# A post-norm transformer block on one core: the window's steps in a new written order, and the causal mask in one product

## The reference

```
qkv    = x @ Wqkv                                   # 16 heads of 16
logits = q k^T / 4 + slope[h] * (j - i), and -inf where j > i
x      = layernorm(x + softmax(logits) v @ Wout)
h      = silu(x @ wg^T) * (x @ wu^T)                # 768 hidden, weights int32 * 1/127
x      = layernorm(x + h @ wd^T)
```

## Time and profile before

| | |
|---|---|
| median of 3 runs | 1958.27 us (1955.96 to 1960.21) |
| span of the profiled execution | 1954.4 us; no time of its own outside the span is recorded for it |
| PE busy | 1867.6 us (96%), 18276 matmuls |
| PEld | 1436.9 us (74%) |
| DVE | 1477.3 us (76%) |
| ACT | 1186.9 us (61%) |
| POOL | 1092.4 us (56%) |
| DMA | 299.27 MB, 153 GB/s in the mean |

### The profile page before, as it was taken

The page is one execution under the profiler, slowest core; times in us unless marked ns, Lnnn a source line. Parts: engine busy times, 40 slices in busy tenths (PEclk is TensorE's granted clock), DMA queues, the critical chain, the costliest instruction groups (busy, mean ns, idle before and its releaser), DMA issues.

```text
span 1954.4 us, 46531 instructions
## 1 busy us (share of the span) xinstructions
PE 1867.6 (96%) x18276; PEld 1436.9 (74%) x18276; DVE 1477.3 (76%) x2521; ACT 1186.9 (61%) x1999; POOL 1092.4 (56%) x2052
## 2 busy tenths in 40 slices
PE   5789999999999999999999999999999999999987
PEld 4556777777777777777787787777787777777676
DVE  5667787777778777778777778877778777778745
ACT  1656666566666666666666666666666666666553
POOL 0234665565565565565565565555565555566566
PEclk7999999999999999999999999999999999999998
DMA  6464554454454444445445455445454455444320
GB/s 221 148 200 142 166 161 148 161 160 153 158 158 159 155 155 159 155 156 166 148 155 175 142 168 161 143 163 165 145 171 157 143 168 163 144 165 150 112 78 28
DMA packets 167931, 299.27 MB, mean 153 GB/s; under 512 B 33920, under 2 KB 88960, under 8 KB 155136
## 3 DMA queue, kind: packets, MB, share of 16 engines
q1 hardware_dynamic: 167520, 295.24, 46.2%
q10 hardware_dynamic: 192, 1.05, 0.2%
HBM read 175.64 MB, written 119.54 MB: 151 GB/s over the span
## 4 chain that ended last, share of the span: by engine, by line
PE 77%; DVE 11%; ACT 7%; POOL 1%; issue 1%; DMA 1%; SPq 1%; POOLq 0%; DVEq 0%; ACTq 0%
PE pair L573 75%; ACT probs L799 5%; DVE row_max L878 4%; DVE row_max L881 4%; DVE x1t_lo L866 2%; PE pair L576 2%; ACT x1t_hi L779 1%; ACT pv_t L807 1%; DVE row_max L883 0%; SPq L514 0%; DMA q_rows<-max_lo 0%; POOL h_lo L1004 0%; DMA probs<-L_attn_Wqkv 0%; POOL x L1030 0%; DVE staged_lo L866 0%
## 5 line engine op out<-in xcount | busy, mean ns | idle before, releaser
L799 ACT ACTIVATE probs<-pair 128x1024 f32<-128x1024 f32 x640 | 620.8, 1030 | 317.1 <-PE pair L573 316.7
L997 POOL TENSOR_SCALAR_AFFINE_SELECT probs<-probs 128x256 f32<-128x256 f32 (+1 forms) x896 | 380.2, 440 | 641.5 <-ACT probs L799 634.4
L1004 POOL TENSOR_TENSOR h_lo<-h_fulls,h_hi 128x256 fp32r<-128x256 f32 x384 | 277.5, 741 | 112.9 <-ACT h_hi L831 109.9
L573 PE MATMUL pair<-probs,v_ones 128*32 128x512 f32 (+3 forms) x4096 | 328.5, 439 | 4.3 <-ACT probs L799 1.5
L573 PE MATMUL pair<-q_rows,k_rows 64*128 64x512 f32 (+3 forms) x2048 | 315.2, 366 | 10.0 <-DMA q_rows<-max_lo 2.0
L881 DVE TENSOR_REDUCE row_max<-pair 128x2 f32<-128x1024 f32 x256 | 312.4, 1220 | 12.6 <-PE pair L573 8.0
L573 PE MATMUL pair<-k_rows,q_rows 63*128 63x512 f32 (+3 forms) x2048 | 297.3, 347 | 22.4 <-DVE row_max L881 15.0
L883 DVE TENSOR_REDUCE row_max<-pair 128x8 f32<-128x1024 f32 x256 | 311.9, 1218 | 0.0
L573 PEld LDWEIGHTS pair<-k_rows,q_rows 63*128 63x128 f32 x2048 | 165.7, 186 | 167.9 <-DVE row_max L881 81.2
L878 DVE TENSOR_REDUCE row_max<-pair 128x4 f32<-128x1024 f32 x128 | 156.9, 1226 | 124.0 <-PE pair L573 124.0
L823 ACT ACTIVATE h_fulls<-pair 128x256 f32<-128x256 f32 x384 | 144.9, 377 | 147.8 <-PE pair L573 145.6
(11 more groups left out here) (89 smaller groups left out, 3281.6 us busy)
## 6 DMA issues: line engine op xcount, KB each, us to landing
q_rows<-bounce SPq DMA_DIRECT2D x192, 256.0 KB
k_rows<-bounce SPq DMA_DIRECT2D x192, 256.0 KB
bounce<-staged_hi SPq DMA_DIRECT2D x128, 256.0 KB, 2.5
bounce<-staged_lo SPq DMA_DIRECT2D x128, 256.0 KB, 2.8
pv_bounce<-pv_t SPq DMA_DIRECT2D x128, 256.0 KB, 2.0
x_sb<-L_attn_x SPq DMA_DIRECT2D x32, 512.0 KB, 4.5
attn<-pv_bounce SPq DMA_DIRECT2D x64, 256.0 KB
recips<-recip_bounce SPq DMA_DIRECT2D x64, 256.0 KB
```

The costliest lines, as they stand in the source:

```text
L573: return tensor.matmul(o, lhs, rhs, start=start, stop=stop, skip_group_check=True, **kw)
L799: scalar.activation(probs[g][:, tile, :, :], pair[:, :, :], ACT.Exp, scale=scale).then_inc(s_exp, 1)
L997: made = pool.affine_select(out=diagonal, in_=diagonal, compare_op=ALU.is_ge, fill=0.0, base=0, pattern=[[0, diagonal.shape[1]], [1, P]], ...
L1004: pool.tensor_tensor(h_lo[:, m, :], h_full[(n_split_h[step] - 1) % H_BUFFERS][:, :], h_hi[:, m, :].bitcast(F32), ALU.subtract).then_inc(s_ ...
```

## The change

The class's `attention` and `rest` are replaced by two tuples, `SEQUENCES`, one for even windows and one for odd ones. A token is a step with its number; "<" in front means that it belongs to the window before (so "<down" in window w is the down of window w-1). There are five differences:

1. The attention stretch now has, between groups of F and S tiles, whole dense steps: both projections of the next unit and the down of the previous window. These were at the end of the rest. The weighted sums are whole (`PV_PARTS` has one part for each group), not in two pieces.
2. All banks go by last use: an F, S or V takes the pair used longest ago, whichever it is, and so do single steps; the pair in which a weighted sum is under way is left out.
3. A V waits for each block's own tile (`LAST_TILE`), not for the last tile of its group.
4. The exponential of H steps (`scores_halved`: two S tiles of an even window, three of an odd one) is two instructions of 512 columns instead of one of 1024, and the next user of each bank waits for its own half.
5. The mask is one product for a whole 128-column block: `turned` and `stair` use powers of two so that 64 rows describe 128 columns. There are two products per tile instead of four, of 128 or 256 columns.

```diff
-PV_PARTS = ((0, 1), (1, 4))
-ATTENTION = ((S, 0), (F, 0), (S, 1), (F, 1), (V, -2, 1, 0), (F, 2), (S, 2), (F, 3), (V, -2, 1, 1), (S, 3), (F, 4), (S, 4),
-             (F, 5), (S, 5), (F, 6), (S, 6), (F, 7), (V, -1, 0, 0), (F, 8), (S, 7), (V, -1, 0, 1), (S, 8), (F, 9), (S, 9))
+PV_PARTS = (((0, 1, 2, 3),), ((0, 1, 2, 3),))
+LAST_TILE = (2, 3, 4, 3)
+SEQUENCES = (
+    (
+        "F 0", "<project 0", "<fetch_recip", "F 1", "S 0", "<load_residual", "<second_norms", "S 1", "V 2 1 0", "S 2", "F 2", "S 3",
+        "F 3", "S 4", "<project 1", "S 5", "F 4", "F 5", "<down", "H 6", "F 6", "S 7", "F 7", "V 1 0 0", "gather", "store_max 0",
+        "divide", "H 8", "S 9", "F 8", "F 9", "combine", "x 0", "gate_up 0", "gate_up 1", "attn_split", "gate_up 2", "x 1",
...
+    ),
+    (
+        "<norm1_later 2", "<project 0", "F 0", "F 1", "H 0", "V 2 1 0", "S 1", "F 2", "S 2", "F 3", "norms", "<stats1 2", "S 3", "S 4",
+        "<project 1", "S 5", "F 4", "F 5", "<down", "<norms", "H 6", "S 7", "F 6", "F 7", "V 1 0 0", "H 8", "F 8", "S 9", "divide",
+        "F 9", "gather", "store_max 1", "x1 0", "x1 1", "store_max 0", "recip", "values 0", "combine", "max_row 0", "values 2",
...
+    ),
+)
...
+    def oldest_pair(self):
+        return min((i for i in range(BANKS // 2) if i != self.held), key=lambda i: max(self.used[2 * i:2 * i + 2]))
...
-                    for c in range(2):
-                        made = both(lambda s: halves[:, s, masked, c, :], lambda r: turned[r:r + HALF, c, :],
-                                    lambda r: stair[r:r + HALF, 0:n, :], False, c == 1)
+                    made = both(lambda s: diagonals[:, s, masked, :], lambda r: turned[r:r + HALF, :],
+                                lambda r: stair[r:r + HALF, 0:n, :], False, True)
...
-                    e.wait_ge(s_select, n_select["select", u, g * TILES + TILES - 1])
                     e.wait_ge(s_values, n_values["values_out", b, 2])
-                    for j in range(*PV_PARTS[part]):
+                    for j in PV_PARTS[g][part]:
+                        e.wait_ge(s_select, n_select["select", u, g * TILES + LAST_TILE[j]])
...
+                    if (u, i) in plan.halved:
+                        for s in range(2):
+                            scalar.activation(probs[g][:, tile, s, :], pair[:, s, :], ACT.Exp, scale=scale).then_inc(s_exp, 1)
```

More of the change, by code:

```diff
@@ L90, in __init__ @@
         self.order, self.norms_due, self.stats_due = [], [], []
-        self.banks, self.before = {}, {}
+        self.banks, self.before, self.halved = {}, {}, set()
         self.user, self.used = [None] * BANKS, list(range(-BANKS, 0))
-        for w in range(-2, self.units + 5):
-            self.attention(w)
-            self.rest(w)
+        for w in range(-2, self.units + 6):
+            self.held = None
+            for token in SEQUENCES[w % 2]:
+                what, *key = token.lstrip("<").split()
+                STEPS[what](self, w - token.count("<"), *map(int, key))
         self.second_norms()
@@ L103, in occupy @@
         self.banks[step] = banks
-        self.before[step] = list(dict.fromkeys(self.user[i] for i in banks if self.user[i] is not None))
+        self.before[step] = [(self.user[i], i % 2) for i in banks if self.user[i] is not None]
         for i in banks:
@@ L118, in norms, with combine, gather, divide @@
         self.norms_due = []
-    def second_norms(self):
+    def combine(self, w):
+        if self.has(w):
+            self.add("combine", w)
+    def gather(self, w):
+        if self.has(w + 1):
+            self.add("gather", w + 1)
+    def divide(self, w):
+        if self.has(w - 3):
+            self.add("divide", w - 3)
+        if w == 0:
+            self.add("load_ffn_weights")
+    def max_row(self, w, with_ffn):
+        if self.has(w) and with_ffn == (self.ffn(w) is not None):
+            self.split("max_row", w)
@@ L121, in second_norms @@
+    def second_norms(self, w=None, with_ffn=None):
+        if with_ffn is not None and with_ffn != (self.ffn(w) is not None):
+            return
         for b, part in self.stats_due:
@@ L125, in second_norms @@
         self.stats_due = []
[L127 to L174, removed]
-        for c in range(2):
[L176 to L201, removed]
-                self.add("split_h", b, part, m - 1)
-    def down(self, b, part):
-        self.take("down", b, part)
-        self.add("residual2", b, part)
-        self.stats_due.append((b, part))
@@ L239, in rest, with recip @@
             self.add("attn_lo", w - 3)
-        if part == 1 and has_ffn:
-            self.max_row(w)
-        if has_ffn and self.has(w):
-            self.add("store_max", w)
+    def recip(self, w):
         if self.has(w - 2):
@@ L461, in bank_emptied @@
             if step[0] == "scores":
-                return s_exp, n_exp[("exp",) + step[1:]]
+                return s_exp, 2 * n_exp[("exp",) + step[1:]] - (side == 0 and step[1:] in plan.halved)
             return s_lo, n_lo[("split_lo",) + step]
@@ L585, in _ @@
                 kind, key = step[0], step[1:]
-                for user in plan.before.get(step, []):
-                    e.wait_ge(*bank_emptied(user))
+                for user, side in plan.before.get(step, []):
+                    e.wait_ge(*bank_emptied(user, side))
                 if kind in ("x", "x1"):
```

234 lines of the change are left out of this document (142 added, 92 removed), and 2 rows, old and new, of the table SEQUENCES.

## The result

The changed kernel takes 1898.53 us in the median (1897.17 to 1901.88, 4 runs) against 1958.26 (1955.96 to 1960.21): the ratio is 0.970, 95% interval 0.9686 to 0.9713. Forecast was 1900. The profiled execution's span is 1900.1 us. That is the slowest of its four executions, 1.6 us above the median, while the span before, 1954.4, is 3.9 us under its median; so the two spans lie 54.3 us apart and the medians 59.7.

What follows compares the result with a forecast made beforehand. PE waiting in a DVE-PE bank chain in attention, alternating with PE alone in the rest, was taken as the bound; 0.97 us a window over 60 windows gave 58 us, 1958 - 58 = 1900 us (own range 1873 to 1928; 8 in 10: 1862 to 1946).

Steps and rivals of the forecast that it cites:

- The bound: Attention stretch: a chain between DVE's reads and PE's bank refills; 10.65 us of PE work takes 13.64, 2.99 waits and restarts.
- The sum of a window: Stretches of 18.4 us, rests of 9.3 and 9.4, plus 0.4 a window: 56.3 us a pair against 58.24.
- borders: Changes between tiles and other work in the new stretch: five pieces at 0.2 us, 1.0 a window, giving 17.35 without waits.
- The walk: Pass through a pair of windows in the changed order of waits and bank releases: stretches end at about 18.4 us.
- Whole sums: Weighted sums whole, V waiting by block: nothing for itself, as the group's last tile is several tiles earlier anyway.
- Halves: Exponentials in two halves: 0.4 us more on ACT a window, banks free 0.5 us earlier; -10 to +10 us by itself.
- Mask: Mask merged from 2560 products to 1280 with the same columns: +2 to -5 us, taken as 0.
- Banks by age: Every bank given by last use, as the walk assumed; no size of its own was forecast.
- Start and end: First and last windows: the down comes one window later, which matters only for the last; plus or minus 6 us.
- third rival: Gather lands late for F 0, slower than before: 1993 us; chance 0.09, shared with any other new hold-up.
- the waits did not come back elsewhere: Rival for the new stretch: tile groups pay another 0.15 us each, only 14 us gained, 1944; chance 0.17.
- One sign: DVE in the attention stretch: no idle of over 1 us, with its busy share up to about 78%.

Runs made afterwards that it cites:

- dense_back: Changed kernel with both projections and the down of each window set one behind the other ahead of the first F: 1998.1 us, 1.0211 of the kernel before.
- early_start: Changed kernel with projections of units 0 to 6 still at the end of the window two ahead, from unit 7 as changed: 1884.2 us.
- dense_and_banks: Kernel before with banks by age, and both projections and the down between the tiles from window 6 on: 2045.7 us, 1.0451 of the kernel before.
- v_split: Changed kernel with each weighted sum in two pieces again, S and F tiles between them: 1973.6 us, 1.0091 of the kernel before.
- banks_back: Changed kernel with the old bank rule, two pairs fixed for F, two for S and V: 2168.2 us, 1.1085 of the kernel before.

## Why the prediction was right, and where it was not

**The bound.** Right in the main: PE was held by the readers in the attention stretch, and the weight loads' waits for row maxima fell from 159.5 to 18.2 us. That in this order of tiles the dense work between them does this is borne out by dense_back, which takes it out and loses 3.6 us a pair, more than the whole gain, with 64.9 and 23.6 us of weight loads' waits for maxima back. The size, 2.99 us a window of waits and restarts, stood on a price of 0.233 for an S tile that was taken from a projection. The prediction's own rows have an S at 1028.62 - 1028.30 = 0.32, and the changed kernel has 0.32 (1008.09 - 1007.77) and, behind a projection, 0.34 (1011.66 - 1011.32). For ten such tiles that is some 0.9 us a window, an estimate, that was counted as waits and did not go away.

**The sum of a window.** Right: 56.10 us for a pair against 56.3, with both stretches (18.54 and 18.47 against 18.4) and both rests near; the four are 0.60 us over their bare sums, where 0.8 was allowed. In the parts it is less good. A whole sum is 2.29 us and not 2.43, 0.28 less a window. With it, the bare pieces of a stretch are 16.35 - 0.28 = 16.07 us, so borders and waits together, priced at 1.0 and some 1.05, were 18.54 - 16.07 = 2.47; the two errors partly cancel. Most of the 2.47 are no waits that show: the one recorded on PE in the odd stretch holds it by 0.46 - 0.04 = 0.42 us. The price of a gap ahead of other work is as estimated: 1012.43 - 1012.27 = 0.16 us from the mask to the down, against 0.04 to a tile.

**The walk.** It is on record with its results and not step by step, so it can't be shown which of its steps gave the value, and 0.8 of its 56.3 us are an allowance. Its waits for ACT are in the trace, at S 4 in the even window and at S 3 instead of S 4 in the odd one. The waits of 0.2 to 0.3 at F 9 and the first step of the rest are not recorded as waits of PE.

**The single edits** are where the prediction failed, behind a right total. Whole sums: "nothing for itself", measured 75 us for their undoing. Halves: within -10 to +10, measured 28.3. Mask: 0, bounds +2 to -5, measured 5 to 8, just outside. Banks by age: counted as a help inside the walk, it is the condition of the new order (270 us) and nothing without it (0.9993). The step that went wrong here is that I priced edits as if they added up. Undone one at a time they cost 3, 6.5, 28, 75, 100, 100 and 270 us, of a gain of 60. In the traces of the five dearest PE waits for readers of banks that the changed kernel does not wait for, or not as long: each one's price is that of an order in which some bank comes round before its reader is done.

**Start and end.** The forecast had 56 windows at 0.97 and half of that for eight more. The trace has 48 windows at 1.07, and 3.0 us in all for the other 16, where the forecast had some 11.6. "Plus or minus 6" was wrong in the parts: some 7 us net lost up to the ninth unit, and about 10 gained behind the 57th, when the 5 us of place are taken out of both. That the total of the medians is met within 1.5 us is in part luck: more in each steady window, less at the ends, and 54.3 us between the spans, in which the 58 were reckoned.

What PE waits for at the start is the third rival's mechanism: too little work between the issue of a gather and the F 0 that needs it, five waits up to 7.7 us, in windows that have no gate_up to cover it. I had looked for it only in the steady part. early_start puts the projections back between the two and takes 12.9 us of these waits and 14.3 us of the time away. Whether the late projection also delays the gather's issue is not shown.

**The rivals.** In the steady part the gather is not waited for, the waits did not come back elsewhere, and some of them stay. ACT's busy time rose by 17.8 us (25 forecast). DVE's busy share of the execution is 77% (78% forecast). One sign failed: no idle of DVE above 1 us was to be in a stretch, and there is one of 1.12 us in the odd and of 1.26 and 1.62 us in the even one.

**What stays open.** Why dense_and_banks loses 88 us is seen in its waits, but not resolved step by step. Of v_split's 75 us the two causes were not separated. Where half of the shorter mask's gain goes, and whether the dense work between tiles gains in any other order of tiles, was not found out.

## What to carry to other kernels

Where a chain between PE and the readers of PSUM alternates with a stretch of PE alone, put the one into the other; but the order and the assignment of banks are one decision. Take the built program, list for each step whose read it waits for, and walk a period with measured durations: that gave 56.3 us for 56.10 here, with 0.8 of allowance in it, while prices for single edits were wrong by 28 and 75 us in the prediction, and by some 230 in the expectation for banks_back. After a reordering look at the filling windows by themselves, since they lack the work that covers a transfer in the steady ones.

## What the runs showed of the hardware that was not expected

From the start of a bf16 mask product of 256 columns to the start of the next float32r product there are 0.04 to 0.05 us where no wait holds it (1011.95 - 1011.90), while 256 columns take 0.12 us in a projection (half of 1.40 / 6). So a distance across such a change of type is not the time of the product in front. Why it is so short is not shown. Distances of whole tiles, from one float32r start to the next, do not cross it: they had the shorter mask at 0.05 us where a tile follows and at 0 where the down does.
